# A gated delta-rule layer with retrieved experts: convolution taps read from the projection's PSUM bank, and v0's taps earlier in VectorE's order

## The chip, the cores and the metric

The kernel runs on one core of a Trainium2 chip. The metric is the device time of one execution in microseconds (us). Engines are named as the profile names them: PE is TensorE's matmul (PEld its weight load), DVE is VectorE, ACT is ScalarE, POOL is GpSimd and SP is SyncE, which here only issues DMAs.

## What is computed

The input is 2048 tokens of width 256 (8 batch rows of 256 tokens, of which the kernel makes 16 tiles of 128). They are normalised, and two branches are added to them. The change touches the attention branch alone. Cut to what matters:

```python
mixed = concat([q, k, v])                # from hidden @ w_qkvz, 16 key heads, 32 value heads
x = conv1d(pad(mixed, 3 left), conv_w)   # four taps, each channel by itself
x = silu(x)
q, k, v = split(x); q = l2norm(q) * DK**-0.5; k = l2norm(k)
def step(state, (q_t, k_t, v_t, g_t, b_t)):      # gated delta rule over the sequence
    state = state * exp(g_t)
    delta = (v_t - state^T k_t) * b_t
    state = state + outer(k_t, delta)
    return state, state^T q_t
xg = out * silu(z)
y = xg * rsqrt(mean(xg*xg) + eps) * norm_w
attention = y @ w_out
ffn = for each token: 8 heads x 8 rows picked from a table of 2048 experts,
      z = silu((h . down_row) * softmax(score)), out = sum z * up_row
return x + attention + ffn
```

## The kernel before

All engines run programs of their own and meet through semaphores; the order on each engine is written by hand. After a routing stage (four groups of tokens) come 64 passes. A pass takes one key head with its two value heads and one group of 512 tokens (two sequences of 256), eight passes to a loop body, and at the end of each body all engines meet at a barrier (`end_pass`).

A pass does two things at once. The *front* prepares the next head: TensorE projects k, q, v0 and v1 (`projection(0)` to `(3)`, L470, each 128 channels x 512 tokens into one PSUM bank, k and v0 into bank 7, q and v1 into bank 6), then z in two halves (`projection(4)` into bank 7, `(5)` into bank 6). ScalarE's `take(u)` (L699) empties each of the first four: L710 copies the bank to the SBUF buffer `raw`, L711 writes the bank times the newest tap's weight to `qkv`. VectorE's `tap(u, d)` (L1073 to L1086, the instruction at L1082) adds the three older tokens' taps, d = 1, 2, 3, in place to `qkv`, each waiting for the one before; the third counts up `conv_v`. ScalarE then takes the SiLU (L715). From k the pass builds a unit triangular matrix for 8 tasks; SyncE moves its 16x16 diagonal blocks through DRAM, and VectorE inverts them by `eliminate` (L1113, 15 short rounds, `xr` and `outer`).

The *back* finishes the head of the pass before: it widens the inverses by three levels (`level_E`, `level_X` on TensorE, `level` on VectorE), and runs the two chunks of each sequence one after the other: `y0_t` product, VectorE's `scaled_y(0)` (L1194, signals `ys0_v`), TensorE's state and output products (L538, "E,Kd" and "E,MT"), `ks_t` products (L615), VectorE's correction of RV (L1214), TensorE's second product ("RV,XT"), `scaled_y(1)`, the last output product ("E,MT"). The output projection (L460) and the gated normalisation lie between. For the experts, GpSimd gathers 16 rows for each token by indirect DMA (L857), VectorE takes dot products (L1098) and a weighted sum (L1110), and adds it to `acc` (L1183, L1185). Other instructions of GpSimd that matter: the product MT (L886), the gating of xg (L834), gate sums gm (L843).

VectorE's order in a pass, which the change edits, is: 16 dots; output of the second chunk (QS L1058, xg L1052); level 0; part of the weighted sum; taps of k; level 1; triangle; taps of q; level 2; sums and `acc`; elimination rounds 0-4; `scaled_y(0)`; rounds 5-10; gated xg (L1052); rounds 11-14 and the transposed copy (L1206, signals `elim_v`); taps of v0; RV correction; two taps of v1; `scaled_y(1)`; the third tap of v1; `add_outputs` (L1047). TensorE's order around it is: `projection(2)`, y0 product, transposes, `projection(3)`, state and output products, output projection, `projection(4)`, `ks_t` products, output projection, "RV,XT", `projection(5)`, "E,MT", and then the next pass's `differences` (L486) and `level_E(0)` (L510).

Of the kernel before, what the change touches and what calls it, by code (L numbers as in the profile page):

```python
# [34 lines left out]
ACT = mybir.ActivationFunctionType  # L35
AX_X = mybir.AxisListType.X

P = 128
# [42 lines left out]
def program(nc, x, wkq, wvz, ckq, cvv, woh, wba, dtb, alog, nw, wup, bup, wdn, bdn, wq, keys, table, consts, out):  # L81
    ctx = ExitStack()
    with ctx:
        def sb(name, shape, dt=F32):
            return ctx.enter_context(nc.sbuf_tensor(name, shape, dt))
# [66 lines left out]
        class Step:  # L152
# [10 lines left out]
            def wait(self, n=None):  # L163
# [3 lines left out]
        per = dict(proj_t=6, diff_t=2, kk_t=2, ss_t=2, e_t=6, x_t=4, xt_t=6, v_t=3, y0_t=1, yt_t=2, s_t=1, o0_t=1, ks_t=2,  # L167
                   y1_t=1, o1_t=1, out_t=2, silu_e=1, exp_done=2, tap_s=8, x_s=4, xt_s=6, silu_s=4, sq_s=2, sumsq_s=8,
                   rv_s=8, S_s=1, qs_s=4, z_s=2, yT_s=2, dot_v=1, xg_v=4, e_v=6, conv_v=4, km_v=1, kq_v=1, ssk_v=2,
# [69 lines left out]
        gm = sb("gm", [P, TASKS, P])  # L239
        raw = sb("raw", [P, 2, N])  # L240
        sq = sb("sq", [P, 2, N])
# [146 lines left out]
        def _(pe):  # L388
# [75 lines left out]
            def one_pass(f, nx, back):  # L464
# [99 lines left out]
                products(0, 6)  # L564
                pe.wait_ge(sm["tap_s"], at("tap_s", 2))
                squares(0, 7)
# [17 lines left out]
                products(1, 7)  # L584
                pe.wait_ge(sm["tap_s"], at("tap_s", 4))
                squares(1, 6)
# [20 lines left out]
                pe.wait_ge(sm["xb_in"], at("xb_in", 16))  # L607
                pe.wait_ge(sm["tap_s"], at("tap_s", 6))
                projection(4)
                if back:  # L610
# [8 lines left out]
                    four(0, 1, lambda b, r, a: XT[:, a, :], RV).then_inc(sm["y1_t"], 1)  # L619
                pe.wait_ge(sm["tap_s"], at("tap_s", 8))  # L620
                projection(5)
# [19 lines left out]
        def _(act):  # L641
# [53 lines left out]
            def one_pass(nx, back):  # L695
# [3 lines left out]
                def take(u):  # L699

                    act.wait_ge(sm["proj_t"], at("proj_t", u + 1))
                    if u == 2:
                        act.wait_ge(sm["w_vz"], at("w_vz", 32))
                    if u >= 2:
                        act.wait_ge(sm["conv_v"], at("conv_v", u - 1))
                    elif place["u"]:
                        act.wait_ge(sm["conv_v"], last("conv_v", u + 3))
                    bank = (7, 6, 7, 6)[u]
                    w = cwkq[:, u, 3:4] if u < 2 else cwv[:, u - 2, 3:4]
                    A(raw[:, u % 2, :], ps[:, bank, :], ACT.Copy).then_inc(sm["tap_s"], 1)  # L710
                    A(qkv[:, u, :], ps[:, bank, :], ACT.Copy, scale=w).then_inc(sm["tap_s"], 1)  # L711
# [202 lines left out]
        def _(dve):  # L914
# [147 lines left out]
            def one_pass(nx, n, st):  # L1062
# [10 lines left out]
                def tap(u, d):  # L1073

                    if d == 1:
                        dve.wait_ge(sm["tap_s"], at("tap_s", 2 * u + 2))
                    else:
                        st.wait(taps[u, d - 1])
                    w = cwkq[:, u, 3 - d:4 - d] if u < 2 else cwv[:, u - 2, 3 - d:4 - d]
                    o = qkv[:, u, :].rearrange("p (b t) -> p b t", b=2)[:, :, d:256]  # L1080
                    i = raw[:, u % 2, :].rearrange("p (b t) -> p b t", b=2)[:, :, 0:256 - d]
                    ins = V.scalar_tensor_tensor(out=o, in0=i, scalar=w, in1=o, op0=ALU.mult, op1=ALU.add)  # L1082
# [95 lines left out]
                if back:  # L1178
# [5 lines left out]
                    st.wait()  # L1184
                    V.tensor_tensor(total, total, mix[:, 1, :], ALU.add).then_inc(sm["mix_v"], 1)  # L1185
                dve.wait_ge(sm["blocks_in"], at("blocks_in", 16))
                dve.wait_ge(sm["zero_p"], at("zero_p", 1))
# [18 lines left out]
                V.tensor_copy(xrT[:, :, :], xr[:, :, :].rearrange("n i c -> n c i")).then_inc(sm["elim_v"], 1)  # L1206
                for d in (1, 2, 3):
                    tap(2, d)
                if back:
# [68 lines left out]
```

## Time and profile before

| | |
|---|---|
| Device time, median of 3 runs | 3936.69 us |
| The three runs | 3885.03, 3936.69, 3954.14 us |
| Span of the profiled execution, first to last instruction | 3551.5 us |
| Own time of the profiled execution | not given apart from its span; the median lies 385.2 us above it |
| Mean granted TensorE clock | 0.935 |
| Passes | 64, in 8 groups of 8 |

The page gives for each engine the time in which it worked. "Idle before, releaser" tells which other engine's instruction ended a wait. An instruction's duration can hold a stall inside it, which then counts as busy time; the shortest against the longest of one kind shows that. A granted clock of 1.00 is 2.4 GHz and 0.50 is 1.2 GHz.

### The profile page before, as it was taken

How to read it: one execution, taken by the hardware profiler on the slowest of the kernel's cores; microseconds unless marked ns; L12 is line 12 of the kernel's file. 1: busy time of each engine (PE TensorE's matmuls, PEld its weight loads, DVE VectorE, ACT ScalarE, POOL GpSimd, SP SyncE). 2: the span in 40 equal slices, each digit the busy share in tenths (PEclk: the TensorE clock that was granted, in tenths of full speed). 3: DMA queues.
4: the chain of work that ended last, by engine and by line, in shares of the span. 5: the costliest groups of instructions: out<-in, count | busy, mean ns of one | idle time of the engine just before them, and what ended most of it. 6: DMA issues, size and time to landing. Idle time of an engine off the chain costs nothing.

```text
span 3551.5 us, 58967 instructions
## 1 busy us (share of the span) xinstructions
PE 3065.3 (86%) x18512; PEld 2458.8 (69%) x18512; DVE 3248.5 (91%) x10343; ACT 1811.4 (51%) x4134; POOL 1861.5 (52%) x1973
## 2 busy tenths in 40 slices
PE   6761799989998899989999898989999899989997
PEld 3330577767777677767777777777777677777776
DVE  7888899989999899989999899989998899989997
ACT  2231455545555455555555555555555555555554
POOL 0001565556665566545665555655556555565555
PEclk8885799999999999999999999999999999999999
DMA  1000555545554455444554454445454454544554
GB/s 58 1 1 25 135 139 137 136 121 147 133 136 129 123 144 133 129 121 134 147 133 132 132 135 133 131 119 141 131 143 127 125 141 130 143 127 137 135 141 136
DMA packets 550338, 435.09 MB, mean 123 GB/s; under 512 B 250976, under 2 KB 457824, under 8 KB 549984
## 3 DMA queue, kind: packets, MB, share of 16 engines
q1 hardware_dynamic: 483424, 226.34, 23.9%
q0 software_dynamic: 66560, 204.54, 20.9%
q8 instruction: 160, 2.62, 0.3%
q14 instruction: 194, 1.59, 0.1%
HBM read 350.93 MB, written 45.74 MB: 112 GB/s over the span
## 4 chain that ended last, share of the span: by engine, by line
DVE 58%; PE 27%; issue 8%; POOL 3%; DMA 3%; DVEq 1%; SPq 1%; ACT 0%; POOLq 0%; ACTq 0%
DVE qkv L1082 12%; PE ps L523 6%; DVE rows L1098 6%; PE ps L510 6%; PE ps L530 6%; DVE mix L1110 5%; DVE outer L1119 5%; DVE xr L1123 5%; PE ps L476 4%; DVE xg L1052 3%; DVE E L1070 2%; DVE acc L1047 2%; POOL rows L857 2%; PE ps L493 2%; DVE acc L1183 2%
## 5 line engine op out<-in xcount | busy, mean ns | idle before, releaser
L857 POOL DMA_INDIRECT rows<-table,pick x1040 | 1047.2, 1007 | 363.9 <-issue 335.7
L715 ACT ACTIVATE qkv<-qkv 128x512 f32<-128x512 f32 x260 | 163.8, 630 | 710.8 <-DVE qkv L1082 710.8
L1082 DVE SCALAR_TENSOR_TENSOR qkv<-raw,cwv,qkv 128x510 f32<-128x510 f32 (+2 forms) x390 | 467.5, 1199 | 6.9
L530 PE MATMUL ps<-XT,E 128*128 128x128 f32 x3072 | 412.2, 282 | 0.0
L510 PEld LDWEIGHTS ps<-X,AT 128*128 128x128 f32 x3072 | 375.4, 197 | 51.0 <-issue 42.3
L523 PEld LDWEIGHTS ps<-E,XT 128*128 128x128 f32 x2048 | 270.0, 202 | 165.1 <-DVE E L1070 132.4
L530 PEld LDWEIGHTS ps<-XT,E 128*128 128x128 f32 x3072 | 381.5, 198 | 0.0
L510 PE MATMUL ps<-X,AT 128*128 128x128 f32 x3072 | 381.2, 278 | 0.3 <-DMA XT<-whole 0.3
L1110 DVE SCALAR_TENSOR_TENSOR mix<-rows,zc,mix 128x256 f32<-128x256 f32 x896 | 374.9, 475 | 0.0
L523 PE MATMUL ps<-E,XT 128*128 128x128 f32 x2048 | 293.2, 289 | 83.6 <-DVE E L1070 83.6
L710 ACT ACTIVATE raw<-ps 128x512 f32<-128x512 f32 x260 | 155.2, 597 | 342.8 <-PE ps L476 342.4
L848 POOL COPY pick<-idx_all 128x16 uint32 (+1 forms) x65 | 12.8, 197 | 562.3 <-DVE E L1070 562.3
L1082 DVE SCALAR_TENSOR_TENSOR qkv<-raw,cwkq,qkv 128x510 f32<-128x510 f32 (+2 forms) x390 | 290.2, 744 | 18.9 <-ACT qkv L711 9.5
L486 PE MATMUL ps<-gm,cst 128*128 128x512 f32 x260 | 192.5, 885 | 123.3 <-issue 57.5
L1098 DVE CUSTOM_DVE_ANT_0 rows<-rows,h2c 128x128 f32<-128x128 f32 x1024 | 257.1, 314 | 42.6 <-issue 37.1
L725 ACT ACTIVATE XT<-ps 128x512 f32<-128x512 f32 x384 | 228.1, 594 | 112.8 <-PE ps L530 104.2
L1070 DVE TENSOR_TENSOR E<-ps,cst 128x512 f32<-128x512 f32 x384 | 253.3, 683 | 27.9 <-PE ps L510 22.6
L476 PE MATMUL ps<-xnT,Wkq 128*128 (+1 forms) x520 | 254.0, 611 | 0.0
L839 POOL COPY gn<-gates 128x8 f32 (+1 forms) x66 | 17.5, 266 | 446.7 <-PE ps L486 312.9
L476 PE MATMUL ps<-xnT,Wvz 128*128 (+1 forms) x520 | 249.5, 603 | 0.0
L538 PE MATMUL ps<-E,MT 128*128 128x128 f32 x1024 | 147.7, 289 | 117.8 <-DVE E L1194 117.8
L460 PE MATMUL ps<-wo,yT 128*128 128x256 f32 x1040 | 246.8, 380 | 0.0
(167 smaller groups left out, 6844.2 us busy)
## 6 DMA issues: line engine op xcount, KB each, us to landing
Wvz<-wvz SPq DMA_DIRECT2D x65, 512.0 KB, 3.2
xb<-xnT SPq DMA_DIRECT2D x65, 512.0 KB, 4.3
whole<-AT SPq DMA_DIRECT2D x130, 256.0 KB
X<-whole SPq DMA_DIRECT2D x130, 256.0 KB, 3.3
XT<-whole SPq DMA_DIRECT2D x130, 256.0 KB, 4.0
Wkq<-wkq SPq DMA_DIRECT2D x66, 256.0 KB, 3.6
rows<-table,pick POOLq DMA_INDIRECT x1040
wo<-woh SPq DMA_DIRECT2D x65, 256.0 KB, 4.0
```

Source lines behind the costliest of these rows:

```text
L460: done = mm(ps[:, 2 + g, c * D:(c + 1) * D], yT[:, task(g, c, r), :], wo[:, r, :], start=r == 0, stop=r == R - 1)
L476: done = mm(ps[:, bank, :], w[:, k, :], xnT[:, k, bass.ds(pn * N, N)], start=k == 0, stop=k == KD - 1)
L486: mm(ps[:, 7 - g, :], mask(C_GT), gm[:, 4 * g:4 * g + 4, :].rearrange("p a i -> p (a i)"), start=True, stop=True).then_inc(sm["diff_t"], 1)
L510: done = mm(ps[:, g, (a % 4) * P:(a % 4 + 1) * P], AT_b[:, a, :], src[:, a, :], start=True, stop=True)
L523: done = mm(ps[:, 2 + g, (a % 4) * P:(a % 4 + 1) * P], src[:, a, :], E[:, a, :], start=True, stop=True)
L530: done = mm(ps[:, 4 + g, (a % 4) * P:(a % 4 + 1) * P], E[:, a, :], src[:, a, :], start=True, stop=True)
L725: return A(dst[:, 4 * g:4 * g + 4, :], ps[:, bank, :].rearrange("p (a i) -> p a i", a=4), ACT.Copy)
L857: pool.indirect_dma_start(rows[:, m, :], None, table[:, :], bass.IndirectOffsetOnAxis(ap=pick[:, m:m + 1], axis=0)).then_inc(gathered, 16)
L1070: V.tensor_tensor(E[:, 4 * g:4 * g + 4, :], ps[:, g, :].rearrange("p (a i) -> p a i", a=4), mask(C_MS + lv, 4), ALU.mult)\
L1082: ins = V.scalar_tensor_tensor(out=o, in0=i, scalar=w, in1=o, op0=ALU.mult, op1=ALU.add)
L1098: st.did(V.tensor_tensor_reduce(out=rows[:, k, 0:P], in0=rows[:, k, 0:P], in1=h2c[:, :], scale=1.0, scalar=0.0, op0=ALU.mult, op1=ALU.add, ...
L1110: sums[s] = st.did(V.scalar_tensor_tensor(out=mix[:, s, :], in0=rows[:, m, P:ROW], scalar=zc[:, 1, m:m + 1], in1=mix[:, s, :], op0=ALU.mul ...
```

## The change

Three things are done. (1) ScalarE's copy to `raw` and the buffer itself are gone; the taps read the PSUM bank. `tap_s` now counts one for each `take`, and `take` no longer waits for a free half of `raw`. (2) So a bank is free only when the taps have read it: TensorE's waits before it overwrites banks 7 and 6 are on `conv_v` (taps done) where they were on `tap_s` (copies done). (3) The three taps of v0 stand ahead of the elimination in VectorE's order, behind the addition to `acc`.

```diff
                 def take(u):
                     act.wait_ge(sm["proj_t"], at("proj_t", u + 1))
...
-                    if u >= 2:
-                        act.wait_ge(sm["conv_v"], at("conv_v", u - 1))
-                    elif place["u"]:
-                        act.wait_ge(sm["conv_v"], last("conv_v", u + 3))
...
-                    A(raw[:, u % 2, :], ps[:, bank, :], ACT.Copy).then_inc(sm["tap_s"], 1)
                     A(qkv[:, u, :], ps[:, bank, :], ACT.Copy, scale=w).then_inc(sm["tap_s"], 1)
...
                     if d == 1:
-                        dve.wait_ge(sm["tap_s"], at("tap_s", 2 * u + 2))
+                        dve.wait_ge(sm["tap_s"], at("tap_s", u + 1))
...
-                    i = raw[:, u % 2, :].rearrange("p (b t) -> p b t", b=2)[:, :, 0:256 - d]
+                    i = ps[:, (7, 6, 7, 6)[u], :].rearrange("p (b t) -> p b t", b=2)[:, :, 0:256 - d]
...
-                pe.wait_ge(sm["tap_s"], at("tap_s", 6))
+                pe.wait_ge(sm["conv_v"], at("conv_v", 3))
                 projection(4)
...
-                pe.wait_ge(sm["tap_s"], at("tap_s", 8))
+                pe.wait_ge(sm["conv_v"], at("conv_v", 4))
                 projection(5)
...
+                for d in (1, 2, 3):
+                    tap(2, d)
                 dve.wait_ge(sm["blocks_in"], at("blocks_in", 16))
                 dve.wait_ge(sm["zero_p"], at("zero_p", 1))
                 eliminate(0, 5)
...
                 V.tensor_copy(xrT[:, :, :], xr[:, :, :].rearrange("n i c -> n c i")).then_inc(sm["elim_v"], 1)
-                for d in (1, 2, 3):
-                    tap(2, d)
```

Two more waits of TensorE, before `squares(0, 7)` and `squares(1, 6)`, change in the same way; each stands behind `products`, which already waits for the SiLU of those taps.

VectorE, from the addition to `acc` to the first rounds of the elimination, before (`outer`, `xr` and `bk` are the elimination's tiles, `cwv` the tap weights of v):

```order
L1185 TENSOR_TENSOR acc<-acc,mix 128x256 [waits step_v]
L1119 TENSOR_TENSOR outer<-bk,xr 64x15 [waits zero_p,blocks_in]
L1123 TENSOR_TENSOR xr<-xr,outer 64x15 [waits step_v]
L1119 TENSOR_TENSOR outer<-bk,xr 64x28 [waits step_v]
L1123 TENSOR_TENSOR xr<-xr,outer 64x14x2 [waits step_v]
```

and the same place after the change:

```order
L1179 TENSOR_TENSOR acc<-acc,mix 128x256 [waits step_v]
L1076 SCALAR_TENSOR_TENSOR qkv1<-ps,cwv,qkv1 128x2x255 [waits tap_s]
L1076 SCALAR_TENSOR_TENSOR qkv1<-ps,cwv,qkv1 128x2x254 [waits step_v]
L1076 SCALAR_TENSOR_TENSOR qkv1<-ps,cwv,qkv1 128x2x253 [waits step_v]
L1113 TENSOR_TENSOR outer<-bk,xr 64x15 [waits zero_p,blocks_in]
L1117 TENSOR_TENSOR xr<-xr,outer 64x15 [waits step_v]
```

Three taps that read `ps` now stand ahead of the elimination and so ahead of `scaled_y(0)`, five rounds later.

TensorE, from the state product of the first chunk to the next pass's `differences`, before (`Kd`, `MT`, `RV`, `XT` and `S` are the back's operands):

```order
L538 MATMUL ps<-E,Kd 128x128 [waits ys0_v]
L480 MATMUL ps<-Wvz,xb 128x256 [waits tap_s,xb_in]
L615 MATMUL ps<-S,qkv0 128x256 [waits S_s]
L538 MATMUL ps<-RV,XT 128x128 [waits r1_v]
L480 MATMUL ps<-Wvz,xb 128x256 [waits tap_s]
L538 MATMUL ps<-E,MT0 128x128 [waits xg_v,ys1_v]
L486 MATMUL ps<-gm,cst 128x512 [waits z_s,gm_p]
```

and after:

```order
L537 MATMUL ps<-E,Kd 128x128 [waits ys0_v]
L479 MATMUL ps<-Wvz,xb 128x256 [waits conv_v,xb_in]
L614 MATMUL ps<-S,qkv0 128x256 [waits S_s]
L537 MATMUL ps<-RV,XT 128x128 [waits r1_v]
L479 MATMUL ps<-Wvz,xb 128x256 [waits conv_v]
L537 MATMUL ps<-E,MT0 128x128 [waits xg_v,ys1_v]
L485 MATMUL ps<-gm,cst 128x512 [waits z_s,gm_p]
```

Nothing moves on TensorE; the second `projection` of these rows (L480, now L479) now waits for the last tap of v1, which VectorE issues behind `scaled_y(1)`.

## Rows read from the trace of the kernel before

**Rows 1.** The profile's page: busy time of each engine.

```profile
PE 3065.3 (86%) x18512; PEld 2458.8 (69%) x18512; DVE 3248.5 (91%) x10343; ACT 1811.4 (51%) x4134; POOL 1861.5 (52%) x1973
```

**Rows 2.** Line L1082, taps of v: ns min/median/max, first and last start.

```profile
L1082 DVE SCALAR_TENSOR_TENSOR qkv<-raw,cwv,qkv x390: 727/745/3743, 382.7 to 3529.3; 128x510 f32<-128x510 f32 x65, 128x506 f32<-128x506 f32 x65, 128x508 f32<-128x508 f32 x65
```

**Rows 3.** Timeline of POOL, one pass (start us, us, engine, line, operation).

```profile
2055.78 2.53 POOL L886 TENSOR_TENSOR MT<-kq,DT 128x512 f32<-128x512 f32 x2
```

**Rows 4.** Line L1058: ns min/median/max, first and last start.

```profile
L1058 DVE TENSOR_TENSOR QS<-ps,QS x65: 675/678/693, 396.8 to 3535.5; 128x512 f32<-128x512 f32 x65
```

**Rows 5.** Groups of VectorE by form (busy us, mean ns, idle before).

```profile
L1092 DVE SCALAR_TENSOR_TENSOR AT<-km,scol,DT 128x128 f32<-128x128 f32 x520 | 147.6, 345 | 2.3
...
L1214 DVE SCALAR_TENSOR_TENSOR RV<-ps,neg,RV 128x128 f32<-128x128 f32 x256 | 71.6, 342 | 0.0
```

**Rows 6.** Timeline of ACT, taking v0 (start us, us).

```profile
2042.55 0.60 ACT L710 ACTIVATE raw<-ps 128x512 f32<-128x512 f32 x1 [1.12 <-PE ps L476]
2043.05 0.68 ACT L711 ACTIVATE qkv<-ps,cwv 128x512 f32<-128x512 f32 x1
```

**Rows 7.** Timeline of DVE, one regular pass (start us, us; merged runs show xN).

```profile
2012.38 0.73 DVE L1082 SCALAR_TENSOR_TENSOR qkv<-raw,cwv,qkv 128x506 f32<-128x506 f32 x1
...
2043.07 0.16 DVE L1119 TENSOR_TENSOR outer<-bk,xr 64x15 f32<-64x15 f32 x1
...
2045.20 0.74 DVE L1194 TENSOR_TENSOR E<-ps,scol 128x256 f32<-128x256 f32 x2
...
2051.59 2.30 DVE L1082 SCALAR_TENSOR_TENSOR qkv<-raw,cwv,qkv 128x510 f32<-128x510 f32 x3
2053.81 1.12 DVE L1214 SCALAR_TENSOR_TENSOR RV<-ps,neg,RV 128x128 f32<-128x128 f32 x4
2054.85 4.50 DVE L1082 SCALAR_TENSOR_TENSOR qkv<-raw,cwv,qkv 128x510 f32<-128x510 f32 x2
2059.27 0.74 DVE L1194 TENSOR_TENSOR E<-ps,scol 128x256 f32<-128x256 f32 x2
2059.93 0.73 DVE L1082 SCALAR_TENSOR_TENSOR qkv<-raw,cwv,qkv 128x506 f32<-128x506 f32 x1
2060.59 1.27 DVE L1047 TENSOR_TENSOR acc<-acc,ps 128x512 f32 x2
```

**Rows 8.** Timeline of PE, the same pass (start us, us).

```profile
2046.00 1.16 PE L538 MATMUL ps<-E,Kd 128*128 128x128 f32 x8
...
2051.34 1.89 PE L615 MATMUL ps<-S,qkv 128*128 128x256 f32 x8
...
2054.98 1.16 PE L538 MATMUL ps<-RV,XT 128*128 128x128 f32 x8
2055.98 1.89 PE L480 MATMUL ps<-Wvz,xb 128*128 128x256 f32 x8
2060.06 1.53 PE L538 MATMUL ps<-E,MT 128*128 128x128 f32 x8 [2.19 <-DVE E L1194]
...
2064.46 1.95 PE L510 MATMUL ps<-X,AT 128*128 128x128 f32 x16
```

**Rows 9.** Busy time of a stretch; the number behind POOL is the granted clock.

```profile
2062.00:2063.00 1.00, 1.00 (x2) 0.34 (x1) 1.00 (x11) 0.00 (x0) 0.00 (x0) 0.50 0.06 20
```

**Rows 10.** Timeline of PE in a pass whose differences ran at full clock.

```profile
2154.63 1.16 PE L538 MATMUL ps<-E,MT 128*128 128x128 f32 x8 [2.19 <-DVE E L1194]
...
2157.39 1.95 PE L510 MATMUL ps<-X,AT 128*128 128x128 f32 x16
...
2164.19 2.08 PE L523 MATMUL ps<-E,XT 128*128 128x128 f32 x8 [3.13 <-DVE E L1070]
```

**Rows 11.** Timeline of DVE, L1058 of two passes that follow each other.

```profile
2161.93 0.69 DVE L1058 TENSOR_TENSOR QS<-ps,QS 128x512 f32<-128x512 f32 x1
...
2212.82 0.69 DVE L1058 TENSOR_TENSOR QS<-ps,QS 128x512 f32<-128x512 f32 x1
```

**Rows 12.** Waits: us in total, times, longest us.

```profile
PE ps L523 <- DVE E L1070: 83.6, 58, 3.2
```

More of the change, by code:

```diff
@@ L167, in program @@
         per = dict(proj_t=6, diff_t=2, kk_t=2, ss_t=2, e_t=6, x_t=4, xt_t=6, v_t=3, y0_t=1, yt_t=2, s_t=1, o0_t=1, ks_t=2,
-                   y1_t=1, o1_t=1, out_t=2, silu_e=1, exp_done=2, tap_s=8, x_s=4, xt_s=6, silu_s=4, sq_s=2, sumsq_s=8,
+                   y1_t=1, o1_t=1, out_t=2, silu_e=1, exp_done=2, tap_s=4, x_s=4, xt_s=6, silu_s=4, sq_s=2, sumsq_s=8,
                    rv_s=8, S_s=1, qs_s=4, z_s=2, yT_s=2, dot_v=1, xg_v=4, e_v=6, conv_v=4, km_v=1, kq_v=1, ssk_v=2,
@@ L239, in program @@
         gm = sb("gm", [P, TASKS, P])
-        raw = sb("raw", [P, 2, N])
         sq = sb("sq", [P, 2, N])
@@ L564, in one_pass @@
                 products(0, 6)
-                pe.wait_ge(sm["tap_s"], at("tap_s", 2))
+                pe.wait_ge(sm["conv_v"], at("conv_v", 1))
                 squares(0, 7)
@@ L584, in one_pass @@
                 products(1, 7)
-                pe.wait_ge(sm["tap_s"], at("tap_s", 4))
+                pe.wait_ge(sm["conv_v"], at("conv_v", 2))
                 squares(1, 6)
```

## The prediction

> **What bounds the kernel now.** I read the page first. VectorE is busy 91% of the span, TensorE 86% [rows 1]: two engines near the limit, so a saving on one can end in a wait for the other. Then I read the timelines of one regular pass. The third tap of v1 starts at 2012.38 and again at 2059.93, a pass of 47.55 us, and VectorE shows no idle time in it worth a name; TensorE's one large gap in this stretch is 2.19 us ahead of its last output product [rows 7, 8]. So VectorE bounds the regular pass. But its busy time holds a stall. A tap of v takes 745 ns in the median and 3743 at most [rows 2]. In the pass shown the first two taps of v1 take 4.50 us instead of 1.50, beside GpSimd's two MT products, 2.53 us from 2055.78 on [rows 3, 7]. A VectorE instruction with one operand in PSUM, L1058, never takes over 693 ns in 65 passes, though GpSimd's gate sums often run beside it [rows 4]. I read from this that what stalls is an instruction with both operands in SBUF.
>
> **ScalarE's copy removed.** It takes 0.60 us [rows 6], four a pass, 260 in all. ScalarE is busy half the span, so most of it is worth nothing. It counts in one place: the taps of v0, which now follow closely on `take(2)`. The weighted copy would begin at 2042.55, where the `raw` copy stood, and end 0.68 us later, 2043.23; with a handoff of some 0.04 us (my reading of the small gaps between engines) the taps can start at 2043.27. VectorE comes to that place at 2043.07, where the elimination begins now [rows 7], and waits 0.20 us.
>
> **Taps from PSUM.** No row shows a tap with PSUM input. The same operation on 128 elements takes 342 ns with one operand in PSUM and 345 with all in SBUF [rows 5], so I price a tap at its old 0.74 us. As bounds I take 0.03 us less and 0.07 us more for a tap, 4% and a tenth, both far beyond the 1% between these two rows: for 12 taps a pass, -0.4 to +0.8 us. What goes for certain is the stall: 4.50 - 1.50 = 3.0 us of VectorE's time a pass. Beside it MT, finished when it is now, is not needed before the next pass.
>
> The Trainium skill, "VectorE: DVE Perf Modes", section on the TRN2 errata, gives a PSUM source a fixed cost of 120 cycles where an SBUF source has 58, so about 65 ns more for each tap; and its rules for kernel authors advise to copy out of PSUM first where many operations follow. By it the change would add 12 x 0.065 = 0.8 us to VectorE's pass. The pair in rows 5 speaks against it; no row shows it at a tap's size.
>
> **Taps of v0 moved.** They leave the stretch behind the elimination and enter the one ahead of it: 2053.81 - 2051.59 = 2.22 us [rows 7]. The sum on VectorE is nil, but `scaled_y(0)` is signalled in the elimination, and TensorE waits for it. Before, its second half ends at 2045.94 and TensorE's state product starts at 2046.00, on the spot [rows 7, 8]: neither waited. Counted from the start of v1's third tap, Y is now ready at
>
> (2043.07 - 2012.38) 30.69 + 0.20 + 2.22 + (2045.94 - 2043.07) 2.87 = 35.98 us.
>
> TensorE is idle for about 2.4 us ahead of it: all else in this stretch of TensorE starts as before. From Y on TensorE sets the time. It goes through state product, output product, output projection, `projection(4)`, `ks_t`, output projection without a gap, 2046.00 to 2054.98 [rows 8], so "RV,XT" starts 9.04 us behind Y and ends 1.16 later, at 10.20; `scaled_y(1)` takes 0.66 to the next start [rows 7], and the third tap of v1 starts at 10.86. VectorE's own work would be there after 2059.93 - 2045.94 - 2.22 - 3.0 = 8.77, so it waits about 2.1 us, part of it for `ks_t`, part for `y1_t`. Sum for a pass with TensorE at full clock: 35.98 + 10.86 = 46.84 us, 0.71 less than now. Of the 3.0 us of stall the larger part goes into waits for TensorE.
>
> **The clock.** TensorE's idle 2.19 us is followed by a granted clock of 0.50, the lower of its two levels, during the differences [rows 8, 9]. From the start of "E,MT" to `level_E` it takes 2064.46 - 2060.06 = 4.40 us there, and 2157.39 - 2154.63 = 2.76 in a pass that kept its clock [rows 8, 10]: the slow stretch costs 1.64 us. Today it falls where VectorE does dots and does not wait. After the change the 2.4 us of idleness stand ahead of the state product, and the slow stretch then lies on the path: 46.84 + 1.64 = 48.48 us. The same 2.19 us left the clock up in the pass of rows 10, so not every gap does it. I choose 6 passes in 10: 0.6 x 48.48 + 0.4 x 46.84 = 47.82, or 0.27 over the regular pass; 64 passes give +17 us.
>
> **TensorE's wait for bank 6.** `projection(5)` ran from 2055.98 in the shadow of the stall; now it waits for v1's third tap. Behind it TensorE's queue holds "E,MT", the differences and `level_E(0)`. From the end of that tap: 0.05 + 1.73 (a block of 1.89 less its overlap) + 2.76 = 4.5 us to `level_E(0)`, against 2064.46 - 2060.66 = 3.8 now. VectorE has add_outputs, dots and QS, some 7 us, ahead of level 0, so I cost it at nothing inside a loop body. It shows at the end of each body, where all engines meet: TensorE ends some 2.8 us behind the tap, where VectorE ends at 1.2; +1.6 us, eight times, +13 us. If the clock falls a second time there, see the second rival.
>
> **Passes that are slow today.** L1058 starts 64 intervals apart in 3535.5 - 396.8 us [rows 4], a mean of 49.04, 1.49 over the regular pass. Barriers hold a part. Another part is passes like that of rows 10: the differences run at full clock, gate sums fall on the dots, and TensorE then waits 3.13 us for level 0 and goes on at the lower clock. Two such L1058 starts are 50.89 apart [rows 11]. TensorE waited 83.6 us in 58 waits at that place [rows 12]; if the ordinary ones are about 0.6 and the long ones 3.1, some 20 are long. At about 2.1 us each (between 1 and 3.3 by the pass) they cost 42 us. After the change `level_E(0)` comes 0.7 us later than the tap's end had it, the gate sums fall behind the dots, and that gap closes. -42 us, the softest term.
>
> **Sum.** +17 + 13 - 42 = -12 us on a span of 3551.5. The profile gives no own time beside the span; the median is 385.2 us above it, and I leave that unchanged: 3936.7 - 12 = 3925 us. A difference of under 2%, 79 us, is about what a measurement here can't tell from none.
>
> **Rivals.**
> 1. *VectorE stays the bound.* Then all of the stall is won: 64 x 3.0 = 192 us, 3745 us. For it: 91% busy, no idle time. Against it: TensorE starts on the spot at 2046.00 and runs gapless to 2054.98 [rows 8]. A milder form: the gap ahead of the state product never lowers the clock, 64 x (46.84 - 47.55) + 13 - 42 = -74, 3862. Chance together 0.20.
> 2. *A second slow stretch* (slower). The idle time ahead of `projection(5)`, 0.66 + 0.73 us and handoffs, 1.5 in all, makes the clock fall too. Then `projection(5)`, "E,MT", differences and `level_E(0)` run late by 1.6 us more; level 0 waits, and with it taps of k. Pass: 48.48 + 1.6 = 50.1; 64 x 2.55 + 13 - 42 = +134, 4070 us. It decides if more than four passes in ten do it. Against it: the idle time is shorter than the 2.19 us of rows 8. Chance 0.17.
> 3. *Taps cost more from PSUM*, by the upper bound, 0.8 us a pass where VectorE is on the path, say 0.6: +38 us, 3963. Chance 0.10.
>
> My forecast has 0.53. Range: 3840 to 4020 us. Faster by over 2%: 0.19 (rival 1 and the low end). Slower: 0.20 (rival 2, and the forecast with the clock low in every pass and the 42 us not won). Same: 0.61.
>
> **What would show it.** Right: taps at 0.74 us without a long one; the state product ("E,Kd") behind a wait of about 2.4 us for VectorE's L1194 line; VectorE with waits of 0.7 us for `ks_t` and above 1 us for `y1_t`; the granted clock low behind Y in about half of the passes; passes of 46.8 and 48.5 us; VectorE's busy share down to about 86%. Wrong: no wait of TensorE ahead of "E,Kd" (rival 1), a low clock in the differences beside one behind Y (rival 2), a tap above 0.8 us (rival 3), or the 3.1 us gap ahead of `level_X(0)` still in twenty passes (the 42 us).

## The result and the profile after

The changed kernel took 4082.86 us in the median of four runs (4078.56 to 4095.97), the kernel before 3944.86 beside it (3885.03 to 3954.14): a ratio of 1.0417, 95% interval 1.0368 to 1.0465. It is slower, and the forecast of 3925 us (3840 to 4020) was wrong. Ratios here and below leave out executions more than 1.5% above the fastest of the same kernel, which matters most for e1 to e4, where the kernel before took 3958.58 to 4001.10 us three times and 4073.95 to 4083.34 four times.

The page of the changed kernel, busy time of each engine, and below it the shares of the chain that ended last (the profiled execution took 4078.56 us):

```profile
PE 3302.6 (81%) x18512; PEld 2681.8 (66%) x18512; DVE 3196.7 (78%) x10343; ACT 1718.6 (42%) x3874; POOL 1798.2 (44%) x1973
...
PE 40%; DVE 36%; another core or an unknown queue 7%; DMA 6%; issue 6%; SPq 2%; ACT 1%; PEldq 1%; DVEq 0%; POOL 0%; POOLq 0%; PEld 0%; ACTq 0%
```

VectorE fell from 91% to 78% [rows 1]: 52 us less work, in a span 525 us longer. The v taps alone are 178 us less (467.5 to 289.5), so some 126 us came back in other instructions, most of them in the elimination, as told below. The taps answer to [rows 2] (ns min/median/max):

```profile
L1076 DVE SCALAR_TENSOR_TENSOR qkv<-ps,cwv,qkv x390: 726/746/750, 376.7 to 4054.0; 128x510 f32<-128x510 f32 x65, 128x506 f32<-128x506 f32 x65, 128x508 f32<-128x508 f32 x65
```

The maximum is 750 ns where it was 3743, so the stall is gone from the taps, and a PSUM tap costs what an SBUF tap did. The waits of the changed kernel (us in total, times, longest) answer to [rows 12]:

```profile
DVE E L1064 <- remote: 176.3, 51, 4.8
DVE qkv L1076 <- ACT qkv L705: 149.9, 60, 8.4
PE ps L537 <- DVE E L1190: 142.5, 58, 3.6
ACT RV L762 <- remote: 133.9, 48, 3.6
PE ps L479 <- DVE qkv L1076: 109.3, 66, 5.6
```

The third and the fifth are the two waits that the forecast named. The two that say "remote" have nothing to do with the change. They are waits that end long after the work which should end them, and the trace of before has no such row. The timeline of the changed kernel shows one (start us, us):

```profile
2021.73 1.06 PE L522 MATMUL ps<-E,XT 128*128 128x128 f32 x8
...
2023.12 0.60 ACT L719 ACTIVATE XT<-ps 128x512 f32<-128x512 f32 x1 [1.49 <-PE ps L529]
...
2025.99 0.60 ACT L719 ACTIVATE X<-ps 128x512 f32<-128x512 f32 x1 [2.27 <-remote]
2028.88 0.60 ACT L719 ACTIVATE XT<-ps 128x512 f32<-128x512 f32 x1 [2.29 <-remote]
```

By the profile, which models the ends of matmuls, the X product ends at 2022.79, and ScalarE, idle since 2023.72, takes it at 2025.99, 3.20 us later; the XT product behind it ends at 2023.68 and is taken at 2028.88, 5.20 us later. I call these late signals below. The name is my reading: an engine whose instructions come late would look the same, and TensorE too sits idle longer for no reason that the profile shows (ahead of its weight loads of L475 206.1 us here, 129.5 in e13 below). I take them for the reason why the span of 3551.5 us in the trace of before and the median of 3936.69 us differ by 385: the two don't come from like executions. e1 bears that out, a trace of before with late signals and a span of 3937.4 us.

### The profile page after: what moved, and what is told of

It reads as the page before. It is cut to its first block, busy times and chain, and to the rows that moved or that the text cites. A ratio compares the mean times of both kernels' runs of the same rounds, so it can differ in the third digit from the quotient of the medians.

```text
span 4076.7 us, 58530 instructions
## 1 busy us (share of the span) xinstructions
PE 3302.6 (81%) x18512; PEld 2681.8 (66%) x18512; DVE 3196.7 (78%) x10343; ACT 1718.6 (42%) x3874; POOL 1798.2 (44%) x1973
## 4 chain that ended last, share of the span: by engine, by line
PE 40%; DVE 36%; another core or an unknown queue 7%; DMA 6%; issue 6%; SPq 2%; ACT 1%; PEldq 1%; DVEq 0%; POOL 0%; POOLq 0%; PEld 0%; ACTq 0%
PE ps L475 8%; PE ps L509 8%; DVE outer L1113 7%; PE ps L529 7%; DVE qkv L1076 6%; DVE xr L1117 5%; PE ps L522 4%; DMA XT<-whole 4%; PE ps L492 3%; PE ps L499 3%; DMA whole<-xrT 2%; PE ps L479 2%; DVE AT L1086 2%; DVE mix L1104 2%
## 5 line engine op out<-in xcount | busy, mean ns | idle before, releaser
L529 PE MATMUL ps<-XT,E 128*128 128x128 f32 x3072 | 460.9, 302 | 12.4 <-issue 12.3
L1104 DVE SCALAR_TENSOR_TENSOR mix<-rows,zc,mix 128x256 f32<-128x256 f32 x896 | 442.6, 551 | 0.0
L1076 DVE SCALAR_TENSOR_TENSOR qkv<-ps,cwv,qkv 128x510 f32<-128x510 f32 (+2 forms) x390 | 289.5, 742 | 161.1 <-ACT qkv L705 141.6
L479 PE MATMUL ps<-Wvz,xb 128*128 128x256 f32 x1040 | 310.9, 452 | 109.3 <-DVE qkv L1076 109.3
L1113 DVE TENSOR_TENSOR outer<-bk,xr 64x15 f32<-64x15 f32 (+7 forms) x975 | 324.2, 333 | 26.8
L475 PE MATMUL ps<-xnT,Wvz 128*128 (+1 forms) x520 | 300.8, 710 | 50.9 <-DVE kq L1169 50.9
L479 PEld LDWEIGHTS ps<-Wvz,xb 128*128 128x128 f32 x1040 | 227.8, 225 | 160.4 <-DVE qkv L1076 118.2
L1076 DVE SCALAR_TENSOR_TENSOR qkv<-ps,cwkq,qkv 128x510 f32<-128x510 f32 (+2 forms) x390 | 290.1, 744 | 17.5 <-ACT qkv L705 8.4
L475 PE MATMUL ps<-xnT,Wkq 128*128 (+1 forms) x520 | 253.1, 609 | 0.0
L716 ACT ACTIVATE z<-ps 128x512 f32<-128x512 f32 x130 | 77.8, 598 | 403.3 <-PE ps L479 403.3
L1117 DVE TENSOR_TENSOR xr<-xr,outer 64x15 f32<-64x15 f32 (+7 forms) x975 | 219.2, 225 | 33.4
```

Source lines behind the costliest of these rows:

```text
L475: done = mm(ps[:, bank, :], w[:, k, :], xnT[:, k, bass.ds(pn * N, N)], start=k == 0, stop=k == KD - 1)
L479: done = mm(ps[:, bank, (t % 2) * 256:(t % 2) * 256 + 256], xb[:, k, t * P:(t + 1) * P], Wvz[:, k, 2 * P:4 * P], start=k == 0, stop=k == K ...
L529: done = mm(ps[:, 4 + g, (a % 4) * P:(a % 4 + 1) * P], E[:, a, :], src[:, a, :], start=True, stop=True)
L1104: sums[s] = st.did(V.scalar_tensor_tensor(out=mix[:, s, :], in0=rows[:, m, P:ROW], scalar=zc[:, 1, m:m + 1], in1=mix[:, s, :], op0=ALU.mul ...
L1113: made = st.did(V.tensor_tensor(o, bk[:, j, j + 1:BL].unsqueeze(2).broadcast_to([NB * TASKS, BL - 1 - j, j + 1]), xr[:, j:j + 1, 0:j + 1]. ...
L1117: last_row[0] = st.did(V.tensor_tensor(v, v, o, ALU.subtract))
```

## Experiments

The jobs ran on several chips, and the kernel before itself differs among them: 4073.95 us (e1 to e4) and 3985.20 us (e5 to e8) on two, 3570.77 (e9 to e12), 3591.60 (e13 to e16) and 3582.47 (e17, e18) on three others. I call the first two late chips and the other three prompt chips. Each chip was used once, so a chip can't be told from its hour. Each ratio is against before on the same chip.

**e1, e2: before and after again, unchanged.**

> The kernel before, unchanged. The trace that the prediction rests on has a span of 3551.5 us, while its timed executions took 3885 to 3954. Theory A (the profiled execution was an exception): the new span lies within 1% of the time, near 3940, and the first half of a pass (from QS L1058 to kq L1175) takes more than the 19.5 us of the old trace. Theory B (the profile always lies some 385 us below the time for this kernel): span near 3550 again.

> The changed kernel, unchanged. Both theories: time near 4083 us. Theory of late signals: consumers of TensorE's results start 1 to 3 us behind the recorded end of the matmul again, in most passes, and passes take 55 to 58 us. If that was an accident of one execution, passes of 47 to 49 us and a span near 3600.

Before took 4012.06 us in this list and 3958.58 to 4083.34 beside it; after 4084.5, ratio 1.0251 (1.0177 to 1.0324), which isn't clear of the bound of 2%. After repeats to 0.1%, before spreads over 3%, and its longest executions take as long as after. The trace of e1 has the late signals too, with no change in it:

```profile
DVE xg L1052 <- remote: 149.1, 53, 5.1
DVE E L1070 <- remote: 144.0, 54, 4.9
ACT RV L768 <- remote: 100.7, 35, 3.5
ACT XT L725 <- remote: 76.3, 40, 4.7
```

and its v taps are busy for less than in the trace that the forecast read (line, shapes, count, busy us, mean ns, idle before; first the trace of before, then e1):

```profile
L1082 DVE SCALAR_TENSOR_TENSOR qkv<-raw,cwv,qkv 128x510 f32<-128x510 f32 (+2 forms) x390 | 467.5, 1199 | 6.9
```

```profile
L1082 DVE SCALAR_TENSOR_TENSOR qkv<-raw,cwv,qkv 128x510 f32<-128x510 f32 (+2 forms) x390 | 362.1, 929 | 6.9
```

At 0.745 us each, 390 taps are 290.6 us. The stall in them was 177 us in the forecast's trace and is 72 us here. It is not gone, it hits other instructions. I counted over the traces what every VectorE instruction took above the shortest tenth of its form, where that was over 0.2 us and GpSimd's MT product ran beside it. By this count the stall beside MT is 182 us in the forecast's trace, 179 of it in the v taps; in e1 it is 132 us, 71 in the v taps and 61 in the elimination, whose instructions also have both operands in SBUF. The 31 passes inside the loop bodies of e1 that have it in the taps take 52.5 us in the mean, the 25 that have it in the elimination 57.6.

**e3, e4: the two halves of the change, on a late chip.**

```diff
# e3: the change without the move (PSUM taps and their waits)
-                for d in (1, 2, 3):
-                    tap(2, d)
                 dve.wait_ge(sm["blocks_in"], at("blocks_in", 16))
...
                 V.tensor_copy(xrT[:, :, :], xr[:, :, :].rearrange("n i c -> n c i")).then_inc(sm["elim_v"], 1)
+                for d in (1, 2, 3):
+                    tap(2, d)
# e4: the kernel before, with the move alone (raw copy kept)
```

> Taps read PSUM, the raw copy is gone and TensorE waits for the taps, but the taps of v0 stay behind the elimination. Theory 1 (the moved taps cost, by putting TensorE behind scaled_y): faster than the changed kernel by about 2 us a pass, 130 us, near or below the kernel before. Theory 2 (the bank held by the taps costs: projection 4 now waits for taps that come behind the elimination, ks_t and the RV correction behind it, and projection 5 waits for the last tap): slower than the changed kernel, 2 us a pass or more, above 4200.

> Only the taps of v0 move ahead of the elimination; raw stays, and TensorE waits for the copies as before. Theory 1 (the move costs): slower than before by 2.2 us a pass at most less what the MT stall gives back, 3950 to 4080. Theory 2 (the PSUM bank costs): within 1% of the kernel before, 3900 to 3980.

PSUM alone: 4427.16 us, 1.1117 (1.1023 to 1.1210). Move alone: 4040.1 us, 1.0126 (1.0039 to 1.0214), again within the bound of 2%. Without the move, `projection(4)` waits for taps behind the elimination, and TensorE's whole queue with it.

**e5, e6: both kernels without the gathers of expert rows.** The sums over experts are made from zeros, so a part of the result is left out.

```diff
-                        pool.indirect_dma_start(rows[:, m, :], None, table[:, :],
-                                                bass.IndirectOffsetOnAxis(ap=pick[:, m:m + 1], axis=0)).then_inc(gathered, 16)
+                        pass
...
-                    dve.wait_ge(gathered, 256 * n + 256)
```

> The kernel before without GpSimd's gathers of expert rows (the rows stay zero, so the experts' part is left out). Theory L (engines' signals are late by 1 to 3 us while many DMA packets are under way, and gathers are a main part of them): the time falls by more than GpSimd's own work explains, to 3600 or below, and the pass to 47 to 49 us. Theory M (late signals have nothing to do with the gathers): the time stays within 2% of the kernel before.

> The changed kernel, likewise without the gathers. If my sum on the dependences holds once signals are on time (theory L), this lies within 1.5% of the kernel before without gathers, most likely 0.3% below it. If the change costs through the waits for the PSUM banks whatever the signals do, it lies 2 to 4% above it.

3425.03 and 3576.74 us, 0.8601 (0.8562 to 0.8641) and 0.8987 (0.8945 to 0.9028) of the full kernel before. The late signals go with the gathers: no wait in either trace says "remote", on a chip whose before took 3985 us. The change costs 152 us here, 4.4% of e5. The v taps have no stall to win here, since without gathers GpSimd does its MT products early, from 2027.63 to 2030.17 in a pass whose v1 taps start at 2038.74. The stall stands in the elimination instead, where two instructions of otherwise 0.20 us take 0.67 and 1.21. The v taps of e5 (busy us, mean ns), and below them that place:

```profile
L1081 DVE SCALAR_TENSOR_TENSOR qkv<-raw,cwv,qkv 128x510 f32<-128x510 f32 (+2 forms) x390 | 289.6, 743 | 6.9
```

```profile
2028.33 0.67 DVE L1118 TENSOR_TENSOR outer<-bk,xr 64x60 f32<-64x60 f32 x1
2029.03 1.21 DVE L1122 TENSOR_TENSOR xr<-xr,outer 64x60 f32<-64x60 f32 x1
```

By the count above the stall beside MT is 96 us in e5 and 53 in e6, all of it in the elimination. So this pair shows the price of the change with little of its prize.

**e7, e8: the round trip of the diagonal blocks through memory cut to one partition** (the blocks' data is left out). It tested whether its small packets make the signals late.

```diff
-                sp.dma_start(bk[:, :, :], diagonal(0)).then_inc(sm["blocks_in"], 16)
+                sp.dma_start(bk[0:1, :, :], diagonal(0, 1)).then_inc(sm["blocks_in"], 16)
```

> The kernel before with the DRAM round trip of the diagonal blocks cut to one partition for each transfer (so some 1/128 of its packets; the inverses are then mostly zero, every instruction and signal stays). Theory L2 (late signals come with the bursts of 512-byte and 64-byte packets of this round trip): the time falls to 3600 or below and signals are recorded in full. If the gathers alone do it: within 2% of the kernel before.

> The changed kernel with the same cut. With signals on time (theory L2): within 1.5% of the kernel before with the cut, TensorE idle for about 2.4 us ahead of the state product (E,Kd). If the change's cost does not depend on the signals: 2 to 4% above it.

4040.23 us, 1.0134 (1.0042 to 1.0226), and 4076.6 us, 1.0248 (1.0197 to 1.0299): nothing gained, and the waits for "remote" are still there in e7 (DVE E L1072 242.7 us in 64 waits). It is not these transfers alone.

**e9, e10: the v0 taps put elsewhere.** Both read PSUM, as the changed kernel does.

```diff
# e9, also e16 and e18
-                for d in (1, 2, 3):
-                    tap(2, d)
                 dve.wait_ge(sm["blocks_in"], at("blocks_in", 16))
...
                     scaled_y(0, 1, "y0_t", "ys0_v")
+                for d in (1, 2, 3):
+                    tap(2, d)
# e10: the same, and
-                for d in (1, 2):
+                for d in (1, 2, 3):
                     tap(3, d)
                 if back:
                     scaled_y(1, 0, "y1_t", "ys1_v")
-                tap(3, 3)
```

> The kernel after the change, with the three PSUM taps of v0 placed right behind scaled_y(0) inside the elimination, so that Y is no longer delayed by them and the projection of v1's bank (L475, u=4) still finds its bank free in time (it starts some 4 us behind Y, the taps end about 2.4 us behind Y). Theory A (the change lost because the moved taps delay Y and with it TensorE, about 2 us a pass, and the rest of the loss is the 1.5 us wait ahead of projection 5): TensorE's wait ahead of 'E,Kd' falls from about 260 us in all to under 60, and the time comes to 3990 to 4040 us, between -1% and +1.5% of before. Rival B (reading the taps from PSUM is itself dear, by what it makes TensorE wait): no gain over the changed kernel, 4080 us, +2 to +3%. Rival C (with signals arriving late nothing of the order matters): also 4080 us, and as many late waits as before.

> As the run before it in this list (v0 taps right behind scaled_y(0)), and v1's third tap stands ahead of scaled_y(1), so that projection 5 waits for nothing and scaled_y(1) comes 0.74 us later. Theory A: the 1.5 us wait ahead of projection 5 goes (109 us of waits at L479 for L1076 in the changed kernel fall to under 20), 'E,MT' stands behind projection 5 anyway, so the 0.74 us cost nothing: 3960 to 4020 us, up to 0.5% below the run before it, and possibly under before itself by 0 to 1%. Rival B: scaled_y(1) is on the path and its 0.74 us return: no difference from the run before it, within 0.4%.

This was the surprise. The chip was prompt (before 3570.77 us), and e9 took 3388.2 us, 0.9491 (0.9453 to 0.9528); e10 3389.15, 0.9499. All three expectations of e9 were wrong by size; theory A had the sign. In e10 TensorE's wait for v1's third tap falls from 108.0 us to 68.0, not under 20 as expected, and the time stays the same (rival B of e10).

**e11, e12: the halves without gathers** (edits of e4 and e3 with that of e5; expert sums from zeros again).

> Leaves out the gathers of expert rows (their sums are made from zeros). Before without gathers took 3425.0 us with passes of 46.0 us, after without gathers 3576.7 with 47.8. This one moves only the taps of v0 and keeps the raw copy, so no projection waits for a tap. If the loss of 152 us is the delayed Y (theory A), this kernel carries most of it: Y comes 2.2 us plus a wait of 1 to 2 us for take(2) later, passes 47.2 to 47.8, 3500 to 3580 us, +2.2 to +4.5% over before without gathers. Rival B (it is the waits for the PSUM banks): 3425 to 3450 us, and 'E,Kd' waits while the pass is no longer.

> Leaves out the gathers of expert rows (their sums are made from zeros). PSUM taps with their waits, the taps of v0 at their old place behind the elimination. With gathers this version took 4427 us, +11% (442 us, 6.9 us a pass). Theory A (projection 4 waits in TensorE's queue for v0's third tap, at the end of the elimination, and what stands behind it comes as late): the same loss without gathers, 6 to 7 us a pass, passes of 52 to 53 us, 3800 to 3880 us. Rival B (a part of the 442 us came from late signals in longer waits): 3600 to 3750 us, passes of 49 to 51 us.

3765.88 and 3737.88 us on the prompt chip, 1.0543 (1.0503 to 1.0582) and 1.0461 (1.0426 to 1.0496) of the *full* kernel before. e5 and e6 ran on another chip, and I don't subtract across chips, so these two say only that each half alone is worse than the full kernel before even with the gathers gone.

**e13 to e16: after, the halves and e9's kernel on one prompt chip.**

> The changed kernel, unchanged. The kernel before takes 3570 us on one chip (no late signals in its trace, as in the profile that the prediction was read from) and 3945 to 4074 us on others (late signals). So what this run says depends on what before takes beside it. If before takes 3550 to 3600 us here: theory P (the prediction's sum holds for the execution that it was read from) says a ratio of 0.99 to 1.01, 3530 to 3600 us; rival Q (the delayed Y and the bank waits cost more than the stall gives, as the pair without gathers said with +4.4%) says a ratio of 1.03 to 1.05, 3680 to 3750 us. If before takes over 3900 us here: 4080 us again, ratio 1.00 to 1.045, and before is the one that varies.

> Only the taps of v0 moved, the raw copy kept. If before takes 3550 to 3600 us here: theory Q (Y delayed by the taps of v0 is the loss, and the raw copy ahead of them makes it later still) says 1.04 to 1.06, 3710 to 3790 us, above the changed kernel, as without gathers (3765.9 against 3576.7 us, though on different chips); theory P says 0.99 to 1.01. If before takes over 3900 us here: 1.00 to 1.02 as in the first run of it.

> Only the PSUM taps and their bank waits, v0's taps behind the elimination. If before takes 3550 to 3600 us here: projection 4 waits at the end of the elimination for v0's third tap in every pass; by the waits without gathers (402 us at L479) less the 3 us stall a pass that goes, 1.05 to 1.08, 3750 to 3850 us. If the stall's end is worth all its 177 us, 1.00 to 1.02. If before takes over 3900 us here: 1.09 to 1.12.

> The taps of v0 right behind scaled_y(0), read from PSUM. Took 3388.2 us, a ratio of 0.949, where before took 3570.8. If before takes 3550 to 3600 us here: 0.945 to 0.955 again. If before takes over 3900 us here: theory (the order matters under late signals as well) 0.95 to 0.98, 3800 to 3950 us; rival (late signals set the time there) 1.00 to 1.03, 4000 to 4090 us.

| beside before, 3591.6 us | us | ratio (95%) |
|---|---|---|
| e13, after | 3613.66 | 1.0103 (1.0041 to 1.0164) |
| e14, move alone | 3728.54 | 1.0403 (1.0349 to 1.0456) |
| e15, PSUM alone | 3736.68 | 1.0438 (1.0381 to 1.0496) |
| e16, PSUM, v0 taps behind `scaled_y(0)` | 3390.84 | 0.9468 (0.9413 to 0.9522) |

On a prompt chip the unchanged after is 1% slower than before, where the late chips gave 4.2% and 2.5%. The halves don't add: each alone costs 4%, both together 1%. The rows show what each costs. First e15, where `projection(4)` stands behind the elimination's end (us in total, times, longest):

```profile
PE ps L479 <- DVE qkv L1076: 371.2, 129, 7.7
DVE RV L1208 <- PE ps L614: 322.2, 64, 5.6
```

then the timeline of e14, move alone, in two places, DVE and below it POOL:

```profile
2030.08 3.63 DVE L1082 SCALAR_TENSOR_TENSOR qkv<-raw,cwv,qkv 128x510 f32<-128x510 f32 x3 [2.04 <-ACT qkv L711]
2035.82 0.74 DVE L1196 TENSOR_TENSOR E<-ps,scol 128x256 f32<-128x256 f32 x2
...
2044.07 4.67 DVE L1082 SCALAR_TENSOR_TENSOR qkv<-raw,cwv,qkv 128x510 f32<-128x510 f32 x2
```

```profile
2030.19 2.98 POOL L834 TENSOR_TENSOR xg<-xg,rms 128x512 f32<-128x512 f32 x2
...
2045.65 2.53 POOL L886 TENSOR_TENSOR MT<-kq,DT 128x512 f32<-128x512 f32 x2
```

The taps of v0, now ahead of Y and with both operands in SBUF, take 3.63 us in this pass instead of 2.3, beside GpSimd's gating of xg, and those of v1 still stall beside MT (2045.65 to 2048.18). In other passes of e14 the elimination does (by the count above 55 us in the v taps, 72 in the elimination). In e13 the same two stand like this:

```profile
2084.58 1.52 DVE L1076 SCALAR_TENSOR_TENSOR qkv<-ps,cwv,qkv 128x510 f32<-128x510 f32 x2
```

```profile
2083.85 2.54 POOL L880 TENSOR_TENSOR MT<-kq,DT 128x512 f32<-128x512 f32 x2
```

MT runs across both taps, and they take 1.52 us. The Trainium skill, "SBUF — State Buffer", section "SBUF: two separate sides", says that VectorE and GpSimd share a pair of ports held for a whole instruction, also by a VectorE instruction with two SBUF inputs. By that rule, the traces agree: 4.67 us with two, 1.52 with one in PSUM.

**e17, e18: the place of the taps or the PSUM source?** e17 is the kernel before with the raw copy kept and v0's taps behind `scaled_y(0)`; e18 is e9's kernel.

> The kernel before with the raw copy kept, and only the taps of v0 placed right behind scaled_y(0). On a chip where before takes 3550 to 3600 us: if the gain of 5.1 to 5.3% in taps_behind_y comes from the place of the taps alone (theory O), 0.94 to 0.96, 3370 to 3450 us. If it comes from the PSUM source, which ends the stall of the v1 taps beside GpSimd's MT products (theory S: 3.0 us in most passes, behind scaled_y(0) where the reordering costs nothing), 0.99 to 1.01, and the taps of cwv keep a busy time of 350 to 470 us. Where before takes over 3900 us: O 0.95 to 0.98, S 1.00 to 1.02.

> The taps of v0 right behind scaled_y(0), read from PSUM, for the pair with e17 on the same chip. Where before takes 3550 to 3600 us: 0.945 to 0.955 a third time. Where before takes over 3900 us: if the order matters under late signals as well, 0.95 to 0.98, 3800 to 3950 us; if late signals set the time there, 1.00 to 1.03, 4000 to 4090 us.

e17 took 3550.17 us, 0.9919 (0.9888 to 0.9950), e18 3386.33 us, 0.9452 (0.9408 to 0.9497). The place alone gives 0.8%, which is within the bound of 2%, and of the 5.5% the rest, 164 us, comes with the PSUM source. The two kernels also differ in ScalarE's `raw` copy and in TensorE's bank waits; no run has the one without the others. The v taps of e17 and of e16 (busy us, mean ns):

```profile
L1082 DVE SCALAR_TENSOR_TENSOR qkv<-raw,cwv,qkv 128x510 f32<-128x510 f32 (+2 forms) x390 | 498.1, 1277 | 9.4 <-ACT qkv L711 2.5
```

```profile
L1076 DVE SCALAR_TENSOR_TENSOR qkv<-ps,cwv,qkv 128x510 f32<-128x510 f32 (+2 forms) x390 | 288.2, 739 | 8.2 <-ACT qkv L705 1.2
```

The difference, 210 us of VectorE's time, is the stall, so 164 of 210 us show in the time. With v0's taps behind Y nothing on TensorE waits for them; the timeline of e16, PE and below it DVE:

```profile
2006.50 1.88 PE L475 MATMUL ps<-xnT,Wvz 128*128 x4
2008.28 1.16 PE L537 MATMUL ps<-E,Kd 128*128 128x128 f32 x8
...
2011.90 1.89 PE L479 MATMUL ps<-Wvz,xb 128*128 128x256 f32 x8
```

```profile
2008.15 2.29 DVE L1076 SCALAR_TENSOR_TENSOR qkv<-ps,cwv,qkv 128x510 f32<-128x510 f32 x3
```

`projection(4)` starts in its turn at 2011.90, and v0's third tap has ended at 2010.44 (2008.15 + 2.29). Nor does the stall turn up elsewhere. VectorE's last step of the elimination and, below it, GpSimd's MT in the same pass:

```profile
2015.83 0.37 DVE L1202 COPY xrT<-xr 64x256 f32<-64x256 f32 x1
```

```profile
2017.58 2.50 POOL L880 TENSOR_TENSOR MT<-kq,DT 128x512 f32<-128x512 f32 x2
```

The elimination is over when MT starts, and what runs beside MT are instructions that read PSUM: by the count above the stall beside MT is 1 us in the whole of e16. Of its 56 passes inside the loop bodies none has the low clock behind "E,Kd"; in e13 44 have. This version beats before by over 5% on the three prompt chips, and after by 6% on the one where both ran. It wasn't run on a late one.

## Why the prediction was wrong, point by point

**Two steps failed.** The first is the last of the sum: "the median is 385.2 us above it, and I leave that unchanged". The 385 us are not a constant laid on top; they are late signals, spread through every pass, and they change which engine waits and what runs beside what. On the prompt chip, whose time is near that of the profile, the difference was +22 us between the medians (1.0103) where -12 was forecast: no change by the bound of 2% and within the range, but on the other side of nought, and for reasons given below. In the scored runs, on a late chip, it was +138, and in e2 2.5%.

The second is "What goes for certain is the stall". It went from the taps and not from VectorE. By the count above the stall beside MT is 182 us in the trace of before and 132 in e1; in the trace of after it is 155, all in the elimination and in every one of the 64 passes, and in e2 158. The elimination of after and, below it, of e16 (busy us, mean ns, idle before):

```profile
L1113 DVE TENSOR_TENSOR outer<-bk,xr 64x15 f32<-64x15 f32 (+7 forms) x975 | 324.2, 333 | 26.8
L1117 DVE TENSOR_TENSOR xr<-xr,outer 64x15 f32<-64x15 f32 (+7 forms) x975 | 219.2, 225 | 33.4
```

```profile
L1113 DVE TENSOR_TENSOR outer<-bk,xr 64x15 f32<-64x15 f32 (+7 forms) x975 | 195.2, 200 | 27.4 <-DMA bk<-whole 0.7
L1117 DVE TENSOR_TENSOR xr<-xr,outer 64x15 f32<-64x15 f32 (+7 forms) x975 | 195.0, 200 | 33.5
```

The same work takes 153 us more in after. One pass of it, VectorE, then GpSimd, then TensorE:

```profile
2047.68 0.88 DVE L1046 SCALAR_TENSOR_TENSOR xg<-ps,rq,z 128x256 f32<-128x256 f32 x2 [3.29 <-remote]
2048.48 2.14 DVE L1113 TENSOR_TENSOR outer<-bk,xr 64x48 f32<-64x48 f32 x1
```

```profile
2048.06 2.49 POOL L880 TENSOR_TENSOR MT<-kq,DT 128x512 f32<-128x512 f32 x2
```

```profile
2053.63 1.16 PE L537 MATMUL ps<-RV,XT 128*128 128x128 f32 x8 [1.41 <-DVE RV L1208]
```

The moved taps put the elimination 2.3 us later, and in its midst the gated xg waits 3.29 us for a late signal; so rounds 11 to 14 come to stand beside MT, one instruction of 0.20 us takes 2.14, and RV and "RV,XT" behind it are late. In e1 31 of the 56 inner passes still had the stall in the taps, and these were the shorter ones; in after none has it there. The inner passes take 56.16 us in the mean against 54.79 in e1, and the last passes of the first seven bodies, ahead of the barriers, 65.5 against 58.0, where the forecast had 1.6 us more at each. The trace of e1 is of the shortest execution in its list, so these differences are the largest that its chip gives. Two more costs stand in the rows: the clock is low behind "E,Kd" in 43 of the 56 passes (none in e1), and the taps of v0 wait longer for ScalarE's copy, 149.9 us against 36.7 in e13:

```profile
DVE qkv L1076 <- ACT qkv L705: 36.7, 64, 8.0
PE ps L537 <- DVE E L1190: 140.5, 60, 2.5
PE ps L479 <- DVE qkv L1076: 109.2, 66, 10.1
```

The waits ahead of "E,Kd" and `projection(5)` are the same on both (142.5 and 109.3 above). How the 138 us divide among these is open; no run switched the late signals off and left all else. What makes them late is open too. They come with the gathers, and only in some of the jobs.

**The steps by themselves**, on e13. First TensorE in a pass at full clock, then VectorE's QS at the start of this pass and of the next two:

```profile
2077.13 1.16 PE L537 MATMUL ps<-E,Kd 128*128 128x128 f32 x8 [2.49 <-DVE E L1190]
...
2085.93 1.05 PE L537 MATMUL ps<-RV,XT 128*128 128x128 f32 x8
2088.48 1.99 PE L479 MATMUL ps<-Wvz,xb 128*128 128x256 f32 x8 [1.50 <-DVE qkv L1076]
```

```profile
2046.44 0.69 DVE L1052 TENSOR_TENSOR QS<-ps,QS 128x512 f32<-128x512 f32 x1
...
2093.47 0.69 DVE L1052 TENSOR_TENSOR QS<-ps,QS 128x512 f32<-128x512 f32 x1
...
2142.70 0.69 DVE L1052 TENSOR_TENSOR QS<-ps,QS 128x512 f32<-128x512 f32 x1
```

- *The stall of 3.0 us*: gone in 32 of the 56 inner passes; in the other 24 it stands in the elimination, 3.0 to 3.1 us each time. One such place, VectorE and below it GpSimd:

```profile
2130.20 3.27 DVE L1117 TENSOR_TENSOR xr<-xr,outer 64x15 f32<-64x15 f32 x1
```

```profile
2130.93 2.50 POOL L880 TENSOR_TENSOR MT<-kq,DT 128x512 f32<-128x512 f32 x2
```

- *Taps from PSUM at 0.74 us*: right, 742 ns in the mean and 746 in the median. Rival 3 falls. The 65 ns a tap that the Trainium skill, "VectorE: DVE Perf Modes", section on the TRN2 errata, would have added don't show.
- *Wait for `take(2)`, 0.20 us*: right on a prompt chip (0.23 in this pass), wrong on a late one.
- *TensorE's idle 2.4 us ahead of "E,Kd"*: 2.49. *Ahead of `projection(5)`*: 1.5 predicted, 1.50.
- *A pass at full clock*, 46.84: 47.03 (2093.47 - 2046.44). *The low clock's price*, 1.64: in the pass of 2142.70 "E,Kd" starts at 2174.16 and "RV,XT" at 2184.61, 10.45 us apart against 8.80 here, 1.65 more.
- *Six passes in ten with it*: too few. Of 56 passes inside the loop bodies 44 take over 11.5 us from Y to `scaled_y(1)`, where a full clock gives 10.68, and the granted clock is low behind "E,Kd" in the same 44. The 24 with the stall in the elimination are among them and take 0.3 to 0.7 us more from Y to `scaled_y(1)` than the other 20. The pass from 2093.47 to 2142.70, 49.23 us, has a granted clock of 0.50 both behind "E,Kd" and behind `projection(5)`:

```profile
2124.50:2125.50 1.00, 1.00 (x6) 1.00 (x6) 0.87 (x4) 0.00 (x0) 0.69 (x2) 0.50 0.63 197
2138.00:2139.00 1.00, 1.00 (x3) 0.82 (x4) 1.00 (x5) 0.33 (x1) 0.00 (x0) 0.50 0.64 189
```

  The second is rival 2's stretch. `projection(5)` runs at the low clock in 22 of 64 passes, under the "more than four in ten" that it needed. In the scored trace it is 34 of 64, over that bound, and the 4070 us of the rival lie close to the 4083 measured; but that is luck in part, since before has it too on a late chip, in 37 of 64 passes of e1, without any wait for the tap.
- *+13 us at the barriers*: right on this chip. The last pass of a body takes 55.80 us in the mean, 54.13 before; eight times 1.67 is 13.
- *-42 us from passes that are slow today*: not won, as the softest term. The inner passes are 48.91 us in the mean against 48.32 before. 20 of 56 still have a first half (QS to `kq`) of over 0.5 us above the median, 17 before.

So +17 + 13 - 42 = -12 became 56 x 0.59 + 13 = +46 us between the two profiled executions (3600.8 - 3551.5 = 49). That the medians come as near to the forecast as 34 us is luck.

- *Rival 1*, all of the stall won, 192 us: wrong for this order, but its size is that of e18, 3582.47 - 3386.33 = 196 us. The forecast's reason against it, that Y would be late and TensorE's gapless run begin later, is what e16 took away: with Y in time and the elimination over before MT, most of the stall's worth is there: 164 us by the source, 32 by the place.

## What to carry to other kernels

When the profiled span is 10% off the runs, find out what the difference is made of before adding a change in microseconds to it; look for waits whose releaser ended long before. When a step is moved ahead of another, ask which signal stands behind it: three taps cost 223 us more ahead of `scaled_y(0)` than behind it (e13 less e16). When a stall between two engines is to be taken away, ask what else will stand beside the other engine's work afterwards: the taps no longer stalled, and the elimination did. And two halves of an edit can each lose 4% and lose 1% together, so a half tried alone is no verdict on the whole.

## What was unexpected of the hardware

The same program takes 3571 to 3592 us on three chips and 3945 to 4074 on others, with signals that seem to land 3 to 5 us late (3.20 and 5.20 us in the rows shown). Without the gathers a late chip shows none of it: 3425 us for before. And a tap with one operand in PSUM beside GpSimd's products took its plain 0.75 us where the same tap with both in SBUF took up to 4.09 (e1).
